# Output bias: eight GpSimd adds or two accumulating transfers into x2

## The reference

```
def bit_linear(x, w, b):
    gamma_x = clip(max(abs(x), axis=-1), 1e-05); scale_x = 127.0 / gamma_x
    x_dq = clip(round(x * scale_x), -128.0, 127.0) / scale_x
    gamma_w = clip(mean(abs(w)), 1e-05); w_dq = clip(round(w / gamma_w), -1.0, 1.0) * gamma_w
    return x_dq @ w_dq.T + b

attention = softmax((c @ Wq.T + bq) @ (c @ Wk.T + bk).T)
x = x + layernorm(x) @ attention.T
h = layernorm(x)
x = x + bit_linear(silu(bit_linear(h, gate_w, gate_b)) * bit_linear(h, val_w, val_b), out_w, out_b)
```

## Time and profile before

| | before |
|---|---|
| time, median of 3 runs | 60.80 us (60.59 to 60.98) |
| the profiled execution's own time | 60.99 us |
| its span, first to last instruction | 59.3 us |
| granted TensorE clock, mean | 1.00 |
| busy: TensorE, VectorE | 51.3 us (87%), 48.2 us (81%) |
| busy: ScalarE, GpSimd | 47.6 us (80%), 44.9 us (76%) |
| data moved | 8.92 MB |

### The profile page before, as it was taken

The page is one execution under the profiler, slowest core; times in us unless marked ns, Lnnn a source line. Parts: engine busy times, 40 slices in busy tenths (PEclk is TensorE's granted clock), DMA queues, the critical chain, the costliest instruction groups (busy, mean ns, idle before and its releaser), DMA issues.

```text
span 59.3 us, 1140 instructions
## 1 busy us (share of the span) xinstructions
PE 51.3 (87%) x298; PEld 32.7 (55%) x301; DVE 48.2 (81%) x122; ACT 47.6 (80%) x84; POOL 44.9 (76%) x102
## 2 busy tenths in 40 slices
PE   1999998899999699929899988899999997979910
PEld 1768866468888478613323634333473752759800
DVE  3249859897999799996998989898999997997150
ACT  0723929989999999979999685999999999798700
POOL 4970002798789888798779978989999999999900
DMA  0789999999993000000002001299270199920573
GB/s 0 161 232 369 409 339 409 408 407 411 397 400 136 0 17 0 0 6 0 6 0 44 0 0 32 57 180 174 51 137 0 31 185 178 242 72 0 176 235 120
DMA packets 11070, 8.92 MB, mean 150 GB/s; under 512 B 7605, under 2 KB 9141, under 8 KB 11065
## 3 DMA queue, kind: packets, MB, share of 16 engines
q1 hardware_dynamic: 10912, 8.72, 47.5%
q10 hardware_dynamic: 152, 0.14, 1.3%
HBM read 6.04 MB, written 1.05 MB: 120 GB/s over the span
## 4 chain that ended last, share of the span: by engine, by line
POOL 30%; PE 26%; issue 17%; DVE 12%; ACT 9%; POOLq 0%; ACTq 0%
POOL h L344 6%; PE psO L940 5%; PE psT L753 5%; POOL r_cols L276 4%; PE psV L763 3%; DVE nmax L467 3%; PE psG L763 3%; PE psH L940 3%; PE psT L778 3%; POOL rstd L311 3%; ACT o_early L723 3%; DVE x L485 3%; POOL pgam L325 2%; POOL res L372 2%; POOL w_int L409 2%
## 5 line engine op out<-in xcount | busy, mean ns | idle before, releaser
L572 DVE TENSOR_REDUCE pmax<-prod 128x1 f32<-128x1024 f32 x8 | 9.7, 1210 | 0.1
L707 ACT ACTIVATE sil<-psG,s_gv 128x1024 f32<-128x1024 f32 x8 | 8.9, 1112 | 0.6 <-PE psG L874 0.2
L556 DVE TENSOR_TENSOR prod<-psV,sil 128x1024 f32<-128x1024 f32 x7 | 8.5, 1221 | 0.9 <-ACT sil L707 0.5
L859 PE MATMUL psG<-ter_gate,hT 128*128 128x512 bf16 x31 | 8.0, 378 | 0.8 <-ACT sil L707 0.7
L886 PE MATMUL psV<-ter_val,hT 128*128 128x512 bf16 x26 | 7.0, 381 | 0.2 <-issue 0.2
L940 PE MATMUL psO<-ter_out,pT 128*128 128x256 bf16 x48 | 6.2, 273 | 0.7 <-ACT o_early L723 0.7
L940 PEld LDWEIGHTS psO<-ter_out,pT 128*128 128x128 bf16 x48 | 4.4, 98 | 2.4 <-DVE pT L599 0.8
L281 POOL TENSOR_SCALAR ve<-mv 128x2 f32<-128x2 f32 (+1 forms) x3 | 0.6, 197 | 6.0 <-DVE mv L463 5.9
L694 ACT ACTIVATE hT<-psH,unshift 128x256 bf16<-128x256 f16 x8 | 3.8, 475 | 1.5 <-PE psH L842 1.4
L859 PEld LDWEIGHTS psG<-ter_gate,hT 128*128 128x128 bf16 x32 | 2.7, 96 | 4.0 <-issue 2.0
L644 ACT ACTIVATE prob<-psT,nmax 128x256 f32<-128x256 f32 x8 | 3.7, 479 | 1.1 <-DVE nmax L467 1.1
(11 more groups left out here) (142 smaller groups left out, 144.9 us busy)
## 6 DMA issues: line engine op xcount, KB each, us to landing
w_gate<-in_w_gate SPq DMA_DIRECT2D x2, 512.0 KB, 5.1
x<-in_x_tok SPq DMA_DIRECT2D x4, 256.0 KB, 6.3
w_val<-in_w_val SPq DMA_DIRECT2D x2, 512.0 KB, 7.2
xt_sb<-in_x_T SPq DMA_DIRECT2D x4, 256.0 KB, 7.8
w_out<-in_w_out SPq DMA_DIRECT2D x2, 512.0 KB, 8.9
out_x<-res SPq DMA_DIRECT2D x8, 128.0 KB, 1.8
ctx_sb<-in_ctx_T SPq DMA_DIRECT2D x2, 128.0 KB, 2.8
ctx_sb<-in_ctx_T SPq DMA_DIRECT2D x1, 256.0 KB, 6.0
```

Source lines behind the costliest of these rows:

```text
L556: nc.vector.tensor_tensor(prod[:, t % P_RING, :], psV[:], sil[:, t % S_RING, :], ALU.mult).then_inc(prod_done, 1)
L572: nc.vector.tensor_reduce(pmax[:, t:t + 1], prod[:, t % P_RING, :], AX.X, ALU.max, apply_absolute_value=True).then_inc(pmax_done, 1)
L707: nc.scalar.activation(sil[:, t % S_RING, :], psG[:], ACT.Silu, scale=s_gv[:, t, 0:1]).then_inc(sil_done, 1)
L859: nc.tensor.matmul(psG[:, c * HC:(c + 1) * HC], hT[:, t, k, :], w_ter[0][:, k * HID + c * HC:k * HID + (c + 1) * HC], start=(k == 0), stop ...
```

## The change

The bias is no longer added by GpSimd's arithmetic into `res`. Instead `x2` itself receives it in place: GpSimd issues two transfers, each from HBM into four tiles of `x2` (128 partitions x 1024 float32, 512 KB), which add what they bring to what is there. Each waits until all four tiles have been centred, because `h` must be made from `x2` without the bias. The bias in HBM is laid out for it as 128 rows of 2048 numbers. The readers behind it (`add_residual` on GpSimd, and `add_shift`, which is `add_bias_shift` without its first half) take `x2` as their source and wait for the transfer's semaphore `x2b_done`. `bo_sb` and its load are gone.

```
-            def add_bias(t):
-
-                pool.wait_ge(x2_done, t + 1)
-                pool.wait_ge(l_bo, 16)
-                nc.gpsimd.tensor_tensor(res[:, t, :], x2[:, t, :], bo_sb[:], ALU.add).then_inc(zb_done, 1)
-
-            def add_bias_shift(t):
-
-                pool.wait_ge(x2_done, t + 1)
-                pool.wait_ge(l_bo, 16)
-                nc.gpsimd.tensor_tensor(res[:, t, :], x2[:, t, :], bo_sb[:], ALU.add).then_inc(x2b_done, 1)
-                pool.wait_ge(x2b_done, t - LATE + 1)
+            def add_bias(i):
+
+                a, e = i * T // 2, (i + 1) * T // 2
+                for t in range(a, e):
+                    pool.wait_ge(centre_done[t], 1)
+                nc.gpsimd.dma_start(x2[:, a:e, :].rearrange("p t d -> p (t d)"), b_out,
+                                    accum_op=ALU.add).then_inc(x2b_done[i], 16)
+
+            def add_shift(t):
+
+                pool.wait_ge(x2b_done[2 * t // T], 16)
                 pool.wait_ge(nmr1_done, 1)
-                nc.gpsimd.tensor_scalar(res[:, t, :], res[:, t, :], nmr1[:, t:t + 1], 1.0, ALU.add,
+                nc.gpsimd.tensor_scalar(res[:, t, :], x2[:, t, :], nmr1[:, t:t + 1], 1.0, ALU.add,
                                         ALU.mult).then_inc(zb_done, 1)
...
             def add_residual(t):
 
                 pool.wait_ge(o_read, t + 1)
-                pool.wait_ge(zb_done, t + 1)
-                nc.gpsimd.tensor_tensor(res[:, t, :], res[:, t, :], o_early[:, t % EARLY, :],
+                pool.wait_ge(x2b_done[2 * t // T], 16)
+                nc.gpsimd.tensor_tensor(res[:, t, :], x2[:, t, :], o_early[:, t % EARLY, :],
                                         ALU.add).then_inc(early_done, 1)
...
-            inverse_parts(1); h_step(2); gamma_h(2); h_round(3); add_bias(2); h_round(4); h_round(5);
-            gamma_p(0); h_round(6); inverse_parts(2); gamma_p(1); p_round_int(0); add_bias(3); gamma_p(2);
-            h_round(7); to_int(2, 0); to_int(2, 1); gamma_p(3); shift_x(); add_bias(4); scale_out(0);
-            add_bias_shift(5); gamma_p(4); p_round_int(3); scale_out(1); add_residual(0); scale_out(2);
-            add_bias_shift(6); scale_out(3); gamma_p(6); add_residual(1); p_round(6); add_bias_shift(7);
+            inverse_parts(1); h_step(2); gamma_h(2); h_round(3); add_bias(0); h_round(4); h_round(5);
+            gamma_p(0); h_round(6); inverse_parts(2); add_bias(1); gamma_p(1); p_round_int(0); gamma_p(2);
+            h_round(7); to_int(2, 0); to_int(2, 1); gamma_p(3); shift_x(); scale_out(0);
+            add_shift(5); gamma_p(4); p_round_int(3); scale_out(1); add_residual(0); scale_out(2);
+            add_shift(6); scale_out(3); gamma_p(6); add_residual(1); p_round(6); add_shift(7);
```

More of the change, by code:

```diff
@@ L74, in xattn_ffn @@
         bias_rows = sb("bias_rows", [P, HC], BF16)
-        bo_sb = sb("bo_sb", [P, D])
         ident = sb("ident", [P, P])
@@ L156, in xattn_ffn @@
         l_xt = [sem(f"l_xt{i}") for i in range(B)]
-        l_bh, l_bo, stored = (sem(n) for n in ("l_bh", "l_bo", "stored"))
+        l_bh, stored = sem("l_bh"), sem("stored")
         c_id, c_half, c_pick, c_fill = (sem(n) for n in ("c_id", "c_half", "c_pick", "c_fill"))
@@ L169, in xattn_ffn @@
             "st1_done", "mv1_done", "ve1_done", "nm1_done", "rstd1_done", "nmr1_done"))
-        st2_done, mv2_done, ve2_done, rstd2_done, cmax_done, x2b_done = (sem(n) for n in (
-            "st2_done", "mv2_done", "ve2_done", "rstd2_done", "cmax_done", "x2b_done"))
+        st2_done, mv2_done, ve2_done, rstd2_done, cmax_done = (sem(n) for n in (
+            "st2_done", "mv2_done", "ve2_done", "rstd2_done", "cmax_done"))
         centre_done = [sem(f"centre_done{t}") for t in range(T)]
@@ L191, in xattn_ffn @@
         pT_ps, o_done, so_done, o_read = (sem(n) for n in ("pT_ps", "o_done", "so_done", "o_read"))
+        x2b_done = [sem(f"x2b_done{i}") for i in range(2)]
         zb_done = sem("zb_done")
@@ L223, in load_w @@
                              (w_gate, w_val, w_out)[w][z]).then_inc(l_w[w][z], 16)
-            def load_bo():
-                sp.dma_start(bo_sb[:], b_out).then_inc(l_bo, 16)
             def turn(t):
@@ L247, in _ @@
             load_ctx(2, 2, 4); load_x(1, 2, 4); load_x(2, 4, 6); load_x(3, 6, 8); load_w(1, 0);
-            load_xt(0, 0, 1); load_xt(1, 1, 2); load_bo(); load_w(1, 1); load_w(2, 0); load_xt(2, 2, 3);
+            load_xt(0, 0, 1); load_xt(1, 1, 2); load_w(1, 1); load_w(2, 0); load_xt(2, 2, 3);
             load_w(2, 1); load_xt(3, 3, 4); turn_r(1); turn_r(2); turn(0); turn(1); turn(2); turn(3); turn(4);
@@ L414, in add_residual @@
                 pool.wait_ge(o_read, t + 1)
-                pool.wait_ge(zb_done, t + 1)
-                nc.gpsimd.tensor_tensor(res[:, t, :], res[:, t, :], o_early[:, t % EARLY, :],
+                pool.wait_ge(x2b_done[2 * t // T], 16)
+                nc.gpsimd.tensor_tensor(res[:, t, :], x2[:, t, :], o_early[:, t % EARLY, :],
                                         ALU.add).then_inc(early_done, 1)
-            std_x(0, 2); normalise(0); normalise(1); to_int(0, 0); std_x(2, 4); std_x(4, 8); add_bias(0);
-            add_bias(1); centre_x2(0); centre_x2(1); std_x2(0); std_x2(1); h_step(0); gamma_h(0); h_step(1);
+            std_x(0, 2); normalise(0); normalise(1); to_int(0, 0); std_x(2, 4); std_x(4, 8);
+            centre_x2(0); centre_x2(1); std_x2(0); std_x2(1); h_step(0); gamma_h(0); h_step(1);
             h_round(0); inverse_parts(0); centre_x2(4); h_round(1); h_round(2); gamma_h(1); std_x2(2);
-            inverse_parts(1); h_step(2); gamma_h(2); h_round(3); add_bias(2); h_round(4); h_round(5);
-            gamma_p(0); h_round(6); inverse_parts(2); gamma_p(1); p_round_int(0); add_bias(3); gamma_p(2);
-            h_round(7); to_int(2, 0); to_int(2, 1); gamma_p(3); shift_x(); add_bias(4); scale_out(0);
-            add_bias_shift(5); gamma_p(4); p_round_int(3); scale_out(1); add_residual(0); scale_out(2);
-            add_bias_shift(6); scale_out(3); gamma_p(6); add_residual(1); p_round(6); add_bias_shift(7);
+            inverse_parts(1); h_step(2); gamma_h(2); h_round(3); add_bias(0); h_round(4); h_round(5);
[3 more added lines that the diff above has]
+            add_shift(6); scale_out(3); gamma_p(6); add_residual(1); p_round(6); add_shift(7);
             scale_out(4); scale_out(5); add_residual(2); add_residual(3); add_residual(4); scale_out(6);
@@ L589, in add_residual @@
                 dve.wait_ge(o_done, t + 1)
-                dve.wait_ge(zb_done, t + 1)
+                dve.wait_ge(zb_done, t - LATE + 1)
                 dve.wait_ge(so_done, t + 1)
@@ L981 @@
         "b_hidden": np.concatenate([np.asarray(L0_ffn_gate_b), np.asarray(L0_ffn_val_b)]).reshape(4, -1),
-        "b_out": np.broadcast_to(np.asarray(L0_ffn_out_b), (128, D)),
+        "b_out": np.broadcast_to(np.tile(np.asarray(L0_ffn_out_b), B * S // 256), (128, B * S * D // 256)),
     }
```

## The result

The changed kernel is slower. Its executions took 63.0, 63.84, 66.12 and 66.15 us, a median of 64.98 us; the kernel before on the same chip had a median of 60.72 us (60.59 to 60.98). The ratio is 1.041, with a 95% interval of 1.034 to 1.048; it is made from the two changed executions that ran at the higher clocks (1.00 and 0.973 on average), since the other two (0.947) took over 1.5% more than the fastest. The forecast was 61.5 us with a range of 60.4 to 62.8: the direction was right, the size was not, and the fastest execution already lies outside the range.

A forecast was written before the change was run, and what follows sets the result against it. No engine was taken as the limit over the whole span; removed GpSimd adds gain nothing. Two issues delay `p_round_int(0)` by 1.47 us, 0.69 after slack: 60.99 becomes 61.68, forecast as a 61.5 us median, range 60.4 to 62.8.

The forecast's parts named there:

- The removed adds are worth nothing: Eight GpSimd adds, 6.0 us of its time: removal by itself gains about 0.1 us, since following instructions wait for other engines.
- The 30% of the chain and its 1.90 us: GpSimd's share of the chain that ended last, and the time of the four removed adds standing on that chain.
- GpSimd is the bound after all: Rival: the chain's 1.90 us of adds comes back, less two issues; at 0.43 us per issue, 59.8 us; chance 0.10.
- The issue costs GpSimd 1.1 us: Each GpSimd transfer issue, estimated between SP's plain-load issue of 0.43 us and its transposing issue of 1.23 us.
- the 0.8 us that the forecast had named as a sign of being wrong: Forecast wrong if GpSimd's next instruction follows a transfer issue within 0.8 us.
- the issue is cheap: Rival: a GpSimd issue costs under 1.06 us, so at most 0.6 us is lost, down to nothing; chance 0.36.
- The sum of 0.69 us through `widen(0)`: Issues delay `p_round_int(0)` by 1.47 us; after slack of 0.66 at ScalarE's `widen(0)` and 0.12 before `silu(6)`, 0.69 remains.
- The transfers themselves: Second transfer, issued at about 36.2, lands before `add_shift(5)` needs it at about 42.9; wait costed at nothing.
- the cover of 1.6 us: Margin of the second transfer before `add_shift(5)`: 5.1 us landing, from a 512 KB load, against 6.7 us available.
- a rival with a chance of 0.08: The second transfer collides with SP's transposes, so `turn(0)` lands later: 62.2 us; chance 0.08.
- GpSimd stalls in `add_shift(5)`: Rival: the second transfer lands over 8.3 us after issue; at 9.5 us it costs 1.2 us more, 62.5 us; chance 0.06.
- The end: VectorE's 1.26 us wait for `s_o(6)` vanishes, but TensorE's last output matmul is late next; gain 0.03 us.

The follow-up runs named there:

- tiny rows: The changed kernel with both accumulating transfers cut to 256-byte rows instead of 4 KB, most of the bias left out: 61.55 us, ratio 1.007 to the kernel before.

## Why the forecast was right in direction and wrong in size

- **The removed adds are worth nothing.** Right. The kernel with neither adds nor transfers runs at 0.999. The 30% of the chain and its 1.90 us were no gain in waiting: at each add the next instruction was tied to VectorE. The rival "GpSimd is the bound after all" falls with that.
- **The issue costs GpSimd 1.1 us.** Nearly right: 1.10 and 0.91 us by the rows, estimated between the two SP issues. The instruction behind starts 0.88 and 0.70 us after the issue's start, a little before the row of the issue ends, and `gamma_p(1)` behind the second takes 0.59 us where it took 0.30; together `p_round_int(0)` came at 37.74. The 0.70 us is under the 0.8 us that the forecast had named as a sign of being wrong. And the rival "the issue is cheap" doesn't fall: its bounds were a C under 1.06, which the second issue meets, and a loss of at most 0.6 us, and with tiny rows the loss is 0.43. What the issues alone cost is what that rival allowed.
- **The sum of 0.69 us through `widen(0)`.** Right as a mechanism, somewhat large in size: with tiny rows it shows as 0.43 us. In the changed kernel itself it is covered: `silu(4)` is already 2.23 us late when `widen(0)` comes, which waits only 0.39 us.
- **The transfers themselves, "I cost the wait at nothing".** This is the step that failed. It asked when the transfer's own data is needed. Its landing took 6.7 us, not the 5.1 us of the nearest row, which used up the cover of 1.6 us (issued at 36.35, landed at about 43.0) and cost a wait of 0.25 us. It did not ask what else was in flight when the transfer was issued. SP's `turn_r(2)`, issued at 35.60 in the kernel before, was 0.8 us from being waited for, and is a transpose by transfer as `turn(0)` is. The forecast looked at the latter only, as a rival with a chance of 0.08, and priced a collision at 0.7 us. Measured: 2.4 us more landing time for `turn_r(2)`, 2.05 us of TensorE's idle time, and 2.3 us of time in the fastest execution. What the rival described happened as well, and larger than it was priced: `turn(0)` landed after 5.1 us in place of 3.2, hidden for the most part behind the first stall. What stood against it, that the data of an issue at 36.2 should be through by 39.5, is answered by the landing at 43.0.
- **The granted clock.** Nothing in the forecast allowed for it. The trace of before shows a clock of 1.00 all through; a new idle stretch of 2.05 us on TensorE was followed by one of 0.50 in the traced execution and, by their mean clocks, in two of the other three, and cost 0.8 to 3.1 us more.
- **The rival "GpSimd stalls in `add_shift(5)`".** It waits 0.25 us, and nothing hangs on it. The price of this rival had a slip: 1.2 us on top of 61.5 are 62.7 us, not 62.5; it touches neither the forecast nor the range.
- **The end.** Right: the wait for `s_o` vanished, and TensorE was late next.

Two statements of the Trainium skill bear on what failed. It says that DMA engines take turns between the queues that have work for them, a packet at a time (DMA: Bandwidth & Descriptors, "Queues, rings and completion order"). The runs agree in direction: beside a load in another queue the transpose of `rT` takes 3.3, 4.8 and 5.3 us in place of 2.4. They don't agree on a share for each queue, since GpSimd's costs more than ScalarE's, and no run put a load of SP's own queue beside this transpose early enough to compare. And its fit for transfers issued by GpSimd ("Anatomy of one DMA"), 3.2 us for 512 KB (an estimate from that page), was cited in the forecast: the accumulating ones landed after 5.7 and 6.7 us, the plain ones after 4.0 and 4.8; the measurements decide.

**What stays open.** Shown: the second transfer causes the stall, its bytes do most of it and its issue little, and the lowered clock behind the stall goes with TensorE's idle time. Not settled: what holds the transposes, since the DMA engines are at a share of 0.18 in part of the wait; why bytes from GpSimd's queue hold a transpose 1.5 to 2 us longer than bytes from ScalarE's, and why an accumulating transfer beside a transpose of `p_int` brings both nearly to a halt (75 to 84 GB/s) while beside `rT` the plain copy is the worse one. That the three different moments of issue matter in themselves was not excluded.

No version beats the kernel before. The best with a transfer in it, the one with only the first and the one with the second issued late, are at 1.003 and 1.005, and with the bias left out altogether it is 0.999.

## What to carry to other kernels

For a new transfer, ask three things: what its issue delays on the issuing engine, when its data is needed, and which transfers are in flight beside it with little slack, transposing ones above all. An engine's share of the chain is no gain until the producer behind each removed instruction has been looked at; here 6 us of adds were worth nothing. And price a new wait on TensorE with a possible loss of clock behind it, which can cost more than the wait.

## What the runs showed of the hardware

- An accumulating transfer of 512 KB (128 rows of 4 KB) issued by GpSimd takes 0.91 to 1.10 us of GpSimd's time whatever its bytes, a plain one 0.62 to 0.79; in the changed kernel and its plain counterpart they land after 5.7 to 6.7 and 4.0 to 4.8 us.
- Such a transfer issued 0.2 us behind SP's transpose of `rT` stretches that from 2.4 to 4.8 us; issued 0.1 us ahead of a transpose of `p_int`, it stretches that from 3.2 to over 10 us, with the DMA engines at a share of 1.04 to 2.18 and 75 to 84 GB/s.
- SP itself is held too: one issue of a transpose, about 1.2 us long, took 5.76 us in that kernel:

```profile
42.51 5.76 SPq L229 DMA_TRANSPOSE pT_int<-p_int  x1
```

- TensorE idle for 2.05 us was followed by a granted clock of 0.50 for some 6 us; with filler matmuls in the same place, no execution of six had a mean clock under 0.995.
